# Splitting the output-projection stage of a transformer layer into two passes, with the layer-norm statistics taken once for all tiles

## What is computed

```python
def _layernorm(x, eps=1e-5):
    m = mean(x, axis=-1); v = var(x, axis=-1)
    return (x - m) / sqrt(v + eps)

def attn(x):                         # 16 heads of 64
    Q, K, V = circulant(x, wq), circulant(x, wk), circulant(x, wv)
    return circulant(softmax(Q @ K.T * 64 ** -0.5) @ V, wo)

def ffn(x):                          # 8 experts, top 2, F = 1408, and a shared one, F = 2816
    scores = softmax(x @ gate_w.T)
    w, i = top_k(scores, 2); w = w / w.sum() * 2.5
    y = sum over e of combine[e] * ((silu(x @ w_gate[e]) * (x @ w_up[e])) @ w_down[e])
    return y + (silu(x @ sw_gate) * (x @ sw_up)) @ sw_down

x = x + attn(_layernorm(x))
x = x + ffn(_layernorm(x))
```

## Time and profile before

| | us |
|---|---|
| three runs | 4991.98, 4997.41, 4998.54 |
| median | 4997.41 |
| the profiled execution's time | 5022.65 |
| its span on the slowest core (core 3) | 5021.1 |
| spans of the eight cores | 4979.7 to 5021.1 |
| median span of cores 0 to 3, granted clock | 5013.8, 0.892 |
| median span of cores 4 to 7, granted clock | 4991.1, 0.899 |
| TensorE, VectorE, ScalarE busy in the span | 4065.6, 1626.2, 1542.3 |

### The profile page before, as it was taken

One profiled execution on the slowest core, in us unless ns is written; L12 is line 12 of the kernel. 1 busy time (PEld: TensorE's weight loads), 2 busy tenths in 40 slices (PEclk: granted clock), 3 DMA queues, 4 the chain that ended last, 5 costly groups with the idle time before them and its releaser, 6 DMA issues.

```text
span 5021.1 us, 58559 instructions; the slowest of 8 cores (4979.7 to 5021.1 us)
## 1 busy us (share of the span) xinstructions
PE 4065.6 (81%) x18656; PEld 1674.5 (33%) x18656; DVE 1626.2 (32%) x2454; ACT 1542.3 (31%) x1630; POOL 86.8 (2%) x107
## 2 busy tenths in 40 slices
PE   1577777777777777753499999999999999999996
PEld 0322222222222222112143434343434343444433
DVE  4322222222222221113333333333343333343334
ACT  3056666665655565632111111111111111111100
POOL 0100000000000000000000000000000000000000
PEclk9988888888888886656699999999999999999987
DMA  6300000000000000021403131222222221222103
GB/s 218 70 1 7 1 7 1 7 1 7 1 7 1 1 1 0 1 59 76 86 7 63 17 55 24 47 33 37 38 32 38 32 39 32 38 38 32 32 1 134
DMA packets 100824, 165.79 MB, mean 33 GB/s; under 512 B 28080, under 2 KB 69056, under 8 KB 100544
## 3 DMA queue, kind: packets, MB, share of 16 engines
q0 software_dynamic: 83072, 94.93, 12.5%
q1 hardware_dynamic: 17472, 67.11, 3.9%
HBM read 240.17 MB, written 16.78 MB: 51 GB/s over the span
## 4 chain that ended last, share of the span: by engine, by line
PE 77%; DVE 10%; ACT 6%; issue 4%; DMA 2%; DVEq 0%; ACTq 0%; POOL 0%; SPq 0%; POOLq 0%
PE psGU L77 31%; PE psD L77 16%; PE psS L77 11%; PE psO L77 10%; PE psP L77 6%; ACT PT L77 5%; DVE invl L77 4%; PE psT L77 1%; PE psC L77 1%; DMA xst<-xf 1%; DVE lscr L77 1%; DVE stg L77 1%; DVE us_sb L77 1%; DMA out<-obuf 1%; DMA co_sb<-co 1%
## 5 line engine op out<-in xcount | busy, mean ns | idle before, releaser
L77 ACT ACTIVATE PT<-psS,consts 128x1024 bf16<-128x1024 f32 x1024 | 1189.3, 1203 | 918.3 <-PE psS L77 845.4
L77 ACT ACTIVATE gs_sb<-psGU 128x512 bf16<-128x512 f32 x440 | 262.7, 597 | 2170.5 <-PE psGU L77 2101.7
L77 PE MATMUL psD<-prod,wdh 128*128 128x512 bf16 x3520 | 798.2, 386 | 77.1 <-DVE prod L77 75.9
L77 PE MATMUL psGU<-xn2T,wgh 128*128 128x512 bf16 x3520 | 852.6, 386 | 0.0
L77 PE MATMUL psGU<-xn2T,wuh 128*128 128x512 bf16 x3520 | 845.0, 384 | 0.0
L77 PE MATMUL psS<-QTp,KTp 64*128 64x512 bf16 x2048 | 601.1, 425 | 116.0 <-ACT PT L77 99.5
L77 PE MATMUL psO<-PT,Vp 128*65 128x512 bf16 x2048 | 595.0, 416 | 19.9 <-ACT PT L77 19.9
L77 DVE TENSOR_TENSOR yacc<-yacc,psD 128x512 f32<-128x512 f32 x608 | 418.1, 688 | 386.4 <-PE psD L77 385.9
L77 PEld LDWEIGHTS psD<-prod,wdh 128*128 128x128 bf16 x3520 | 329.2, 98 | 546.0 <-issue 269.9
L77 DVE TENSOR_TENSOR us_sb<-psGU,ce_sb 128x512 bf16<-128x512 f32 x352 | 243.5, 692 | 793.8 <-PE psGU L77 793.8
L77 PEld LDWEIGHTS psGU<-xn2T,wgh 128*128 128x128 bf16 x3520 | 348.2, 99 | 430.1 <-issue 42.6
(11 more groups left out here) (105 smaller groups left out, 1269.1 us busy)
## 6 DMA issues: line engine op xcount, KB each, us to landing
xst<-xf SPq DMA_DIRECT2D x16, 2048.0 KB, 9.8
wgh<-wg POOLq DMA_DIRECT2D x8, 1536.0 KB, 14.5
wuh<-wu POOLq DMA_DIRECT2D x8, 1536.0 KB, 22.9
wdh<-wd POOLq DMA_DIRECT2D x8, 1536.0 KB, 29.6
wgh<-wg POOLq DMA_DIRECT2D x8, 1280.0 KB, 12.9
wuh<-wu POOLq DMA_DIRECT2D x8, 1280.0 KB, 19.2
wdh<-wd POOLq DMA_DIRECT2D x8, 1280.0 KB, 24.5
xo<-xf SPq DMA_DIRECT2D x4, 2048.0 KB, 10.5
```

Of the source, the lines that this page charges most:

```text
L77: ins = getattr(e, meth)(*args, **kw)
```

## The change

`x1t` gets one buffer of 1024 float32 for each of the 16 tiles in place of two, and `l2s` goes. The loop over chunks keeps the projection, the transposes of `aost`, the add, the store, the sum and the square. psT3 is used as `psT3[T % 2]`, and its transposes wait for the add of tile T−2. The sum and the square go into the columns of `m_sum` and `m_ssq`, the tiles of stage 1, and the square no longer waits for the sum. After the last chunk come six instructions on [128, 16] that make `m_rstd` and `m_negms` for all tiles. A new loop over the 16 tiles then normalises, transposes (again `psT3[T % 2]`) and copies, with the waits of stage 1's second loop. In the diff the waits are written out in the lists.

```diff
--- before.py
+++ after.py
@@ -530,10 +530,9 @@
             co_sb = cc(nc.sbuf_tensor("co_sb", [128, NDT, D], BF16))
             aost = cc(nc.sbuf_tensor("aost", [128, NDT, 512], BF16))
             xo = cc(nc.sbuf_tensor("xo", [128, 8, D], F32))
-            x1t = cc(nc.sbuf_tensor("x1t", [128, 2, D], F32))
+            x1t = cc(nc.sbuf_tensor("x1t", [128, NTO, D], F32))
             xn2st = cc(nc.sbuf_tensor("xn2st", [128, 2, D], BF16))
             sq2 = cc(nc.sbuf_tensor("sq2", [128, D], F32))
-            l2s = cc(nc.sbuf_tensor("l2s", [128, 2, 8], F32))
             psC = [cc(nc.psum_tensor(f"psC{i}", [128, 512], F32)) for i in range(2)]
             psT3 = [cc(nc.psum_tensor(f"psT3{i}", [128, D], BF16)) for i in range(2)]
 
@@ -571,60 +570,63 @@
                 ACO = S.n("aCo")
                 for tt in range(4):
                     T = c * 4 + tt
-                    sl = T % 2
-                    st = lambda i: l2s[:, sl, i:i + 1]
                     for dt in range(NDT):
-                        ws = [("aCo", ACO)]
-                        if T >= 1:
-                            ws.append(("vE2", T))
+                        ws = [("aCo", ACO), ("vAdd", max(0, T - 1))]
                         S.op("tensor", "transpose",
-                             psT3[sl][:, dt * 128:(dt + 1) * 128],
+                             psT3[T % 2][:, dt * 128:(dt + 1) * 128],
                              aost[:, dt, tt * 128:(tt + 1) * 128], identB[:],
                              waits=ws if dt == 0 else (),
                              inc="pT3" if dt == NDT - 1 else None)
-                    S.op("vector", "tensor_tensor", x1t[:, sl, :], xo[:, T % 8, :],
-                         psT3[sl][:], ALU.add,
+                    S.op("vector", "tensor_tensor", x1t[:, T, :], xo[:, T % 8, :],
+                         psT3[T % 2][:], ALU.add,
                          waits=[("pT3", None),
-                                (f"xoL{(T // 4) % 2}", 16 * (T // 4 // 2 + 1)),
-                                ("vN2", max(0, S.n("vN2") - 1)),
-                                (f"stX{T % 2}", 16 * (T // 2))],
+                                (f"xoL{(T // 4) % 2}", 16 * (T // 4 // 2 + 1))],
                          inc="vAdd")
-                    S.op("vector", "reduce_sum", st(0), x1t[:, sl, :], axis=AX.X,
-                         waits=[("vAdd", None), ("vL", None)], inc="vL")
-                    S.op("scalar", "activation", sq2[:], x1t[:, sl, :], AF.Square,
-                         accum_out=st(2),
-                         waits=[("vAdd", None), ("aL", None), ("vL", None)],
-                         inc="aL")
-                    S.op("vector", "tensor_scalar_mul", st(1), st(0), 1.0 / D,
-                         waits=[("vL", None)], inc="vL")
-                    S.op("vector", "tensor_mul", st(3), st(1), st(1),
-                         waits=[("vL", None)], inc="vL")
-                    S.op("vector", "scalar_tensor_tensor", st(2), st(2), 1.0 / D,
-                         st(3), ALU.mult, ALU.subtract,
-                         waits=[("aL", None), ("vL", None)], inc="vL")
-                    S.op("scalar", "activation", st(3), st(2), AF.Ln, bias=C_EPS,
-                         waits=[("vL", None)], inc="aL")
-                    S.op("scalar", "activation", st(4), st(3), AF.Exp, scale=C_NHALF,
-                         waits=[("aL", None)], inc="aL")
-                    S.op("vector", "scalar_tensor_tensor", st(5), st(1), -1.0,
-                         st(4), ALU.mult, ALU.mult, waits=[("aL", None)], inc="vL")
-                    S.op("sync", "dma_start", out=x1s[T], in_=x1t[:, sl, :],
+                    S.op("sync", "dma_start", out=x1s[T], in_=x1t[:, T, :],
                          waits=[("vAdd", None)], inc=f"stX{T % 2}", inck=16)
-                    S.op("vector", "tensor_scalar", xn2st[:, sl, :], x1t[:, sl, :],
-                         st(4), st(5), ALU.mult, ALU.add,
-                         waits=[("vL", None), ("pT4", max(0, T - 1))], inc="vN2")
-                    for dt in range(NDT):
-                        S.op("tensor", "transpose",
-                             psT3[1 - sl][:, dt * 128:(dt + 1) * 128],
-                             xn2st[:, sl, dt * 128:(dt + 1) * 128], identB[:],
-                             waits=[("vN2", None)] if dt == 0 else (),
-                             inc="pT4" if dt == NDT - 1 else None)
-                    S.op("vector", "tensor_copy",
-                         xn2T[:, :, T * 128:(T + 1) * 128],
-                         psT3[1 - sl][:].rearrange("p (dt c2) -> p dt c2", c2=128),
-                         waits=[("pT4", None)], inc="vE2")
+                    S.op("vector", "reduce_sum", m_sum[:, T:T + 1], x1t[:, T, :],
+                         axis=AX.X, waits=[("vAdd", None)], inc="vL")
+                    S.op("scalar", "activation", sq2[:], x1t[:, T, :], AF.Square,
+                         accum_out=m_ssq[:, T:T + 1],
+                         waits=[("vAdd", None), ("aL", None)], inc="aL")
                 if c + 2 < NCH:
                     load_xo(c + 2)
+            s16 = slice(0, NTO)
+            S.op("vector", "tensor_scalar_mul", m_mean[:, s16], m_sum[:, s16],
+                 1.0 / D, waits=[("vL", None)], inc="vS2")
+            S.op("vector", "tensor_mul", m_negms[:, s16], m_mean[:, s16],
+                 m_mean[:, s16], waits=[("vS2", None)], inc="vS2")
+            S.op("vector", "scalar_tensor_tensor", m_rstd[:, s16], m_ssq[:, s16],
+                 1.0 / D, m_negms[:, s16], ALU.mult, ALU.subtract,
+                 waits=[("aL", None), ("vS2", None)], inc="vS2")
+            S.op("scalar", "activation", m_ssq[:, s16], m_rstd[:, s16], AF.Ln,
+                 bias=C_EPS, waits=[("vS2", None)], inc="aS2")
+            S.op("scalar", "activation", m_rstd[:, s16], m_ssq[:, s16], AF.Exp,
+                 scale=C_NHALF, waits=[("aS2", None)], inc="aS2")
+            S.op("vector", "scalar_tensor_tensor", m_negms[:, s16], m_mean[:, s16],
+                 -1.0, m_rstd[:, s16], ALU.mult, ALU.mult,
+                 waits=[("aS2", None)], inc="vS2")
+            STATS2 = S.n("vS2")
+            for T in range(NTO):
+                ws = [("vS2", STATS2)]
+                if T >= 2:
+                    ws.append(("pT4", T - 1))
+                S.op("vector", "tensor_scalar", xn2st[:, T % 2, :], x1t[:, T, :],
+                     m_rstd[:, T:T + 1], m_negms[:, T:T + 1], ALU.mult, ALU.add,
+                     waits=ws, inc="vN2")
+                for dt in range(NDT):
+                    ws = [("vN2", S.n("vN2"))]
+                    if T >= 2:
+                        ws.append(("vE2", T - 1))
+                    S.op("tensor", "transpose",
+                         psT3[T % 2][:, dt * 128:(dt + 1) * 128],
+                         xn2st[:, T % 2, dt * 128:(dt + 1) * 128], identB[:],
+                         waits=ws if dt == 0 else (),
+                         inc="pT4" if dt == NDT - 1 else None)
+                S.op("vector", "tensor_copy",
+                     xn2T[:, :, T * 128:(T + 1) * 128],
+                     psT3[T % 2][:].rearrange("p (dt c2) -> p dt c2", c2=128),
+                     waits=[("pT4", T + 1)], inc="vE2")
             P3 = S.counts()
 
         if "xn2T" in dbga:
```

## The result

The changed kernel is faster, by 1.5%. The ratio of its time to that of the kernel before is 0.9853, 95% interval 0.9841 to 0.9865: with 4997.5 us before, that is 73.5 us less, 67.5 to 79.5. The median of all its nine runs is 4930.6 us; it includes runs made longer by a lower clock on one die, which the ratio leaves out. The forecast was 4929.5 us and a saving of 67.9.

A forecast was written before the change was run, and what follows sets the result against it. A serial chain through all engines, no single engine, bounds the 217.1 us stage; 100.8 + 2.0 + 46.4 = 149.2 us saves 67.9, so 4997.4 becomes 4929.5 us, eight in ten within 4913 to 4948.

The forecast's parts named there:

- What bounds the stage: Stage from projection to router: no engine bounds it, a chain through all does; 217.1 us, and its saving reaches the end.
- First pass: Projection, transposes back, add, sum, square and store over four chunks: 17.5 + 3 × 24 + 11.3 = 100.8 us.
- A chunk: Each later chunk of the projection loop, between first transposes: 24 us taken, from 23.6 to 25.7.
- The wait before the third group: Projection's third matmul group waits for a PSUM buffer evicted behind the fourth square; starts about 12.1 us after first transposes.
- the tail: Last chunk's four tiles after its matmuls, up to the last square: 11.3 us.
- The half rate after an idle gap: Ten projection matmuls at half clock after the third group's wait of 1 to 3 us: a chunk 25.7 us.
- Statistics: Six instructions on 16 columns between the passes replace 96 on one: 2.0 us, exposed.
- Second pass: Normalise, transpose and copy for 16 tiles at 2.90 us each, as in the first layer norm: 46.4 us, exposed.
- A: Rival: next chunk's matmuls give no cover, a chunk costs 28.8 us; saving 53.5 us, 4944 us; chance 0.07.
- B: Rival: projection runs at half clock throughout; about 39 us back, saving 29, 4969 us; chance 0.03.
- C: Rival: more of the feed-forward stage at clock 0.81, 0.19 us lost per microsecond, possibly slower than before; chance 0.04.
- D: Rival: change does nothing because the path leads past the stage, hidden behind weight loads; 4997 us; chance 0.01.

## Why the prediction was right

*What bounds the stage:* right. The stage gave 73.2 us and the runs 73.5; the profiled spans have 68.5, for the 1.3 and 3.4 us named above. What the stage gives up the end gives up, within 5 us.

Two agreements are closer than the reasoning earns. The sum missed the stage's saving by 5.3 us, so the time should have missed by as much: by the ratio it is 4924 us and not 4929.5. That the median stands at 4930.6 and the profiled execution at 4954.1, for 4954.8 forecast, is chance.

*First pass:* forecast 100.8 us, measured 2321.76 − 2224.65 = 97.1; the last sum ends at 2321.76, 0.1 us ahead of the statistics. The first 17.5 us were exact. A tile took 2.45 us, not 2.6: after the sum the next add came at the lower bound, 1.14 us. A chunk took 23.0 us for 24. The wait before the third group was there, but the group started 11.4 us after the first transposes and not 12.1, most of which is the shorter tile, 3 × 0.15 us; and the half-rate matmuls behind it, for which I had allowed 0.4 us, did not come in any of three chunks. The chunk is the term that was mis-sized most, 3 × 1.0 us, and the tail was 0.6 too long.

*The half rate after an idle gap* was the upper bound, 25.7 us for that chunk. After waits of 1.0, 0.5 and 2.7 us the 48 matmuls took 10.52 us, and the same after the waits of 2.4, 2.5 and 1.0 us in the kernel whose square waits for the sum; after the waits of 5.8 to 6.3 us of the experiment with statistics for each tile they took 12.0 to 13.4, up to 2.9 us more. The Trainium skill ("TensorE: Matmul & The Clock Gate", section "HAM oscillation — how this bites in real kernels") describes long gaps, waits of some 3 to 5 us for a DMA between groups of matmuls, behind each of which the clock is at half again. The traces agree with it on the 6 us waits, and the changed kernel has no wait that long between its matmul groups. The bound was for a wait of 1 to 3 us, and there the runs show no loss.

*Statistics:* 2.0 forecast, and 1.9 measured with 0.1 at the edge. *Second pass:* 46.4 forecast, 2368.51 − 2323.78 = 44.7 measured: 2.78 us a tile and not 2.90. Its transposes wait for two semaphores and the first layer norm's for three, which I had not counted; that one wait is worth 0.1 us was shown by taking another away.

*Rivals:* A (no overlap, 53.5 us saved) did not happen; the kernel without overlap saved 55.7 in the stage, with three statistics steps more than A counts. B did not happen: after the first group or two no chunk has half-rate matmuls. C: the stretch at 0.81 is there in both kernels, at the end of the feed-forward stage, and did not grow enough to matter; what starts it no experiment here tried to tell. D (no change) is out, by the interval.

The sum missed the saving of the stage by 5.3 us of 73.2, all on the side of caution: 3.7 in the first pass and 1.7 in the second.

## What to carry to other kernels

When no engine is half busy in a stage, count the hand-overs in one tile and take links out of the tile before looking at any engine: six tiny instructions of 0.15 to 0.3 us each cost 34 us over sixteen tiles here, mostly by order and not by work (7 of the 34 as matmuls at 1.2 GHz behind the longer wait). Batching them needs a buffer for each tile, and the same split then lets the next projection run under the pass. After such a split look at each loop's order again: issuing tile T+1's first step ahead of tile T's last one gave another 21 us for an exchange of two lines.

## What the runs showed of the hardware

- A further semaphore wait, long satisfied and standing behind the one that blocks, costs TensorE 0.1 us: from the start of the normalisation to that of the transposes it is 0.95 us with one wait and 1.05 with two, and in the first layer norm, in the kernel before, 1.06 with two and mostly 1.16 with three (1.16 to 1.33):

```profile
88.41 0.80 DVE L77 TENSOR_SCALAR xnst<-xst,m_rstd,m_negms 128x1024 bf16<-128x1024 f32 x1
89.57 1.01 PE L77 MATMUL psT<-identB,xnst 128*128 128x128 bf16 x8 [1.88 <-DVE xnst L77]
```

- Transposes fed by another engine ran at either clock: 311 ns each at a granted clock of 0.50 (1.2 GHz) where a tile takes 2.78 us (with a wait of 1.77 us before each tile's transposes) or 1.4 us (mostly 0.3 to 0.5 us), and 219 ns (2.4 GHz) where it takes 0.99 us, after the first two tiles, and between the projection's groups.
- The feed-forward stage, TensorE over 95% busy on all eight cores, kept a granted clock of 0.99 over 2000 us, and fell to 0.81 near its end on some cores, in both kernels: before the change cores 2 and 3 stood at 0.81 from 4750 us on, while cores 0 and 1 of the same die stood at 1.00 until 4900. The Trainium skill ("TensorE: Matmul & The Clock Gate", section "Seeing it yourself") would have the whole die at 13/16 some 5 to 20 us after a third core starts such a load, for as long as it lasts; the runs agree on the level, and not on when it comes or that the whole die has it.
